# Loading tokens eight to a partition, and a grouped convolution in 20-row groups with two store queues

## The reference

```python
x = group_norm(x)                       # over groups of 4 channels, one scale and shift per image
x = x + window_attention(x)             # 8 heads, 8x8 windows with dilation 2, projection, roll
y = conv_general_dilated(x, w, (1, 1), 'SAME', feature_group_count=32) + b   # 3x3, NHWC
y = (y - mean(y, (0, 1, 2))) * rsqrt(var(y, (0, 1, 2)) + 1e-5) * gamma + beta
x = x + relu(y)
for w1, b1, w2, b2, w3, b3 in two_sets:  # two residual blocks of scanned 1x1, 3x3, 1x1 convolutions
    x = block(x)
```

## Time and profile before

| | |
|---|---|
| Median of three runs | 2432.0 us |
| Profiled execution, its own time | 2433.68 us |
| Its span in the trace | 2431.9 us |
| TensorE busy | 2062.5 us, 85% of the span |
| VectorE busy | 1672.6 us, 69% |
| ScalarE busy | 1166.5 us, 48% |
| GpSimd busy | 1068.4 us, 44% |
| Mean granted TensorE clock | 0.941 |
| DMA queue q1 | 239.09 MB, 32.5% of 16 engines' span |

### The profile page before, as it was taken

The page is one execution under the profiler, slowest core; times in us unless marked ns, Lnnn a source line. Parts: engine busy times, 40 slices in busy tenths (PEclk is TensorE's granted clock), DMA queues, the critical chain, the costliest instruction groups (busy, mean ns, idle before and its releaser), DMA issues. The chain is left out here.

```text
span 2431.9 us, 75176 instructions
## 1 busy us (share of the span) xinstructions
PE 2062.5 (85%) x30482; PEld 1083.4 (45%) x30482; DVE 1672.6 (69%) x3497; ACT 1166.5 (48%) x2603; POOL 1068.4 (44%) x1234
## 2 busy tenths in 40 slices
PE   5699989988998899859995377787999999999996
PEld 4455555555555555535553123232344443333332
DVE  5588999899899989962324665666667665655653
ACT  5577666666676676632222244333434443433430
POOL 0277777776777677749501442222112221111100
PEclk8799999999999999979997588898999999999997
DMA  8301111111111111112224655655444444444444
GB/s 229 105 26 46 48 34 48 37 47 33 49 35 48 34 48 36 48 43 72 94 95 172 233 184 145 212 172 173 124 140 131 136 133 106 130 118 120 121 100 104
DMA packets 259007, 243.82 MB, mean 100 GB/s; under 512 B 124784, under 2 KB 230512, under 8 KB 258672
## 3 DMA queue, kind: packets, MB, share of 16 engines
q1 hardware_dynamic: 258672, 239.09, 32.5%
HBM read 92.45 MB, written 89.65 MB: 75 GB/s over the span
## 5 line engine op out<-in xcount | busy, mean ns | idle before, releaser
L1226 POOL TENSOR_SCALAR l_x<-l_x,l_scale,l_shift 128x384 f32<-128x384 f32 x192 | 147.5, 770 | 573.8 <-PE banks L1644 573.8
L1602 PE MATMUL banks<-l_a,l_taps 128*32 128x384 f32 x3456 | 331.1, 517 | 60.2 <-ACT l_r L1298 60.2
L435 POOL TENSOR_TENSOR at_prob<-at_prob,at_inv 128x512 f32<-128x512 f32 x288 | 294.2, 1042 | 116.6 <-DVE at_inv L575 111.3
L501 ACT ACTIVATE at_prob<-at_prob 128x512 f32<-128x512 f32 x288 | 181.9, 632 | 307.4 <-DVE at_prob L565 307.4
L1617 PE MATMUL banks<-l_above,l_taps 128*32 128x384 f32 x1728 | 311.7, 494 | 11.3 <-ACT l_above L1313 9.8
L1309 ACT ACTIVATE l_above<-l_below 96x384 f32<-96x384 f32 x144 | 75.5, 524 | 510.5 <-issue 274.9
L1617 PE MATMUL banks<-l_below,l_taps 128*32 128x384 f32 x1728 | 310.7, 495 | 0.0
L617 PE MATMUL banks<-at_xn,at_w 128*64 128x256 f32 x2336 | 286.1, 387 | 1.8 <-ACT at_xn L453 1.4
L1602 PEld LDWEIGHTS banks<-l_a,l_taps 128*32 128x32 f32 x3456 | 122.2, 115 | 243.8 <-issue 243.8
L1474 DVE COPY l_old<-l_a 32x384 f32<-32x384 f32 x576 | 221.7, 385 | 11.5 <-DVE l_bias L1431 0.2
L656 PE MATMUL banks<-const,at_prob 128*128 128x128 f32 x1152 | 183.8, 287 | 51.2 <-POOL at_prob L435 50.1
(11 more groups left out here) (160 smaller groups left out, 3598.0 us busy)
## 6 DMA issues: line engine op xcount, KB each, us to landing
l_x<-both SPq DMA_DIRECT2D x48, 768.0 KB, 4.4
l_rows<-l_r SPq DMA_DIRECT2D x768, 48.0 KB, 2.0
l_work<-both SPq DMA_DIRECT2D x36, 768.0 KB, 5.5
at_k_bd<-at_k SPq DMA_DIRECT2D x584, 32.0 KB, 1.8
load_raw<-in_x SPq DMA_DIRECT2D x36, 512.0 KB, 5.0
both<-c_y SPq DMA_DIRECT2D x96, 192.0 KB
both<-l_x SPq DMA_DIRECT2D x24, 768.0 KB, 3.9
out<-l_x SPq DMA_DIRECT2D x24, 768.0 KB, 4.5
```

Source lines behind the costliest of these rows:

```text
L435: nc.gpsimd.tensor_tensor(prob[i][p][:, :, :], prob[i][p][:, :, :], inv[i][p][:, :].unsqueeze(2).broadcast_to([P, HEADS, WIN]), ALU.mult). ...
L501: nc.scalar.activation(prob[j % 2][p][:, :, :], prob[j % 2][p][:, :, :], ACT.Exp).then_inc(s["exped"], 1)
L1602: last = nc.tensor.matmul(grid(acc(k)[block_rows(c), :]), e[kind_of(k)][:, dy + 1, dx, :], a[:, k % A_RING, rows_, dx:dx + SIDE], start=(d ...
```

## The change

In the load stage each partition now takes eight consecutive tokens, 4 KB, in one piece. TensorE turns the same 288 blocks; ScalarE writes each bank to every eighth run of four tokens, so that `x_res` holds the tokens in order again; VectorE's statistics of a bank-sized piece wait for both halves of the span. The loops are written out, and eight PSUM banks are used in place of six. Attention's weights, bias and tables are loaded at the end of the load stage, on the same queue behind the spans, and attention's waits for them are gone.

In the grouped convolution a group has 20 rows (four tiles of 5 rows, 480 columns), the last of an image 16 rows; there are 5 groups per image, 20 in all. The stores of quarters 0 and 2 are given out by SyncE, those of 1 and 3 by ScalarE right behind its own copy. The weight preparation starts with group 0 in place of group 2.

```diff
-        x_v = x_dram.rearrange("(g i t p) c -> p i t g c", i=LOAD_RING, t=LOAD_T, p=P)
+        x_v = x_dram.rearrange("(g p t) c -> p g (t c)", t=LOAD_T, p=P)
...
-            sp.dma_start(sh.const[:, :], const_dram).then_inc(const_in, 16)
-            with sp.Fori(0, rounds) as g:
-                for i in range(LOAD_RING):
-                    sp.wait_ge(turned, g * CHUNKS + 2 * i + 2)
-                    sp.dma_start(raw[:, i], x_v[:, i, :, bass.ds(g, 1), :].rearrange("p t g c -> p (t g) c"))\
-                        .then_inc(raw_in[i], 16)
+            for n, (tile, dram) in enumerate(first_drams):
+                if n == 1:
+                    for g in range(spans):
+                        i = g % LOAD_RING
+                        if g >= LOAD_RING:
+                            sp.wait_ge(turned, 2 * (g - LOAD_RING + 1))
+                        sp.dma_start(raw[:, i].rearrange("p t c -> p (t c)"), x_v[:, g, :]).then_inc(raw_in[i], 16)
+                sp.dma_start(tile[:, :], dram).then_inc(late_in if n else const_in, 16)
+            sp.wait_ge(late_in, 16 * (len(first_drams) - 1))
...
-                    act.wait_ge(turned, chunk + 1 + CHUNKS)
-                    nc.scalar.activation(sh.x[:, bass.ds(chunk * BANK, BANK)], sh.bank[n][:, :],
-                                         ACT.Copy).then_inc(kept, 1)
+                act.wait_ge(turned, n + 1)
+                out = sh.x[:, g * LOAD_SPAN:(g + 1) * LOAD_SPAN].rearrange("p (n t) -> p n t", t=LOAD_T)
+                nc.scalar.activation(out[:, :, 4 * half:4 * half + 4],
+                                     sh.bank[n % 8].rearrange("p (t n) -> p n t", t=4), ACT.Copy).then_inc(kept, 1)
...
+            for n in range(2 * spans):
+                dve.wait_ge(kept, n // 2 * 2 + 2)
+                nc.vector.bn_stats(sh.stats[:, n * 6:(n + 1) * 6], sh.x[:, n * BANK:(n + 1) * BANK]).then_inc(counted, 1)
...
-            pe.wait_ge(s["w_in"], 48)
...
-    return g // 2 - 1 if g % 2 == 0 and 0 < g <= 2 * PREPARES else None
+    return g // 2 if g % 2 == 0 and g < 2 * PREPARES else None
...
-C1_ROWS = C1_T * TR
-C1_SPAN = C1_T * TILE
-C1_GROUPS = IMG // C1_SPAN
+C1_MOST = BANK // SIDE
+C1_ROWS = C1_T * C1_MOST
+C1_GROUPS = -(-SIDE // C1_ROWS)
+
+
+def c1_rows(g):
+
+    return min(C1_MOST, (SIDE - g % C1_GROUPS * C1_ROWS) // C1_T)
+
+
+def c1_span(g):
+    first = g // C1_GROUPS * IMG + g % C1_GROUPS * C1_ROWS * SIDE
+    return slice(first, first + C1_T * c1_rows(g) * SIDE)
...
-                for r in range(4):
+                for r in (0, 2):
                     sp.wait_ge(s["y_kept"], 4 * g + r + 1)
-                    sp.dma_start(y_dram[quarter(r), g * C1_SPAN:(g + 1) * C1_SPAN].rearrange("j (c n) -> c j n", c=C1_T),
-                                 y[:, g % Y_RING, r, :]).then_inc(y_out[g % Y_RING], 16)
+                    sp.dma_start(y_dram[quarter(r), c1_span(g)].rearrange("j (c n) -> c j n", c=C1_T),
+                                 y[:, g % Y_RING, r, 0:c1_rows(g) * SIDE]).then_inc(y_out[g % Y_RING], 16)
...
+                    if r % 2:
+                        act.wait_ge(s["y_kept"], 4 * g + r + 1)
+                        nc.scalar.dma_start(y_dram[quarter(r), c1_span(g)].rearrange("j (c n) -> c j n", c=C1_T),
+                                            y[:, g % Y_RING, r, 0:n]).then_inc(y_out[g % Y_RING], 16)
...
                     if n == len(taps) // 2 and prepare_at(g) is not None:
-                        pe.wait_ge(s["y_kept"], 4 * g)
+                        if g:
+                            pe.wait_ge(s["y_kept"], 4 * g)
+                        else:
+                            pe.wait_ge(s["tables"], 1)
...
-                link(nc.vector.bn_aggr(y_agg[:, r_, :], sh.stats[:, r_ * per_kind * 6:(r_ + 1) * per_kind * 6]))
+                link(nc.vector.bn_aggr(y_agg[:, r_, :], sh.stats[:, r_ * per_block * 6:(r_ + 1) * per_block * 6]))
```

More of the change, by code:

```diff
@@ L178, in _ @@
+            sp.wait_ge(late_in, 16 * (len(first_drams) - 1))
         @block.tensor
         def _(pe):
-            pe.sem_inc(turned, CHUNKS)
             pe.wait_ge(const_in, 16)
[L182 to L192, removed]
+            for n in range(2 * spans):
+                g, half = n // 2, n % 2
+                if half == 0:
+                    pe.wait_ge(raw_in[g % LOAD_RING], 16 * (g // LOAD_RING + 1))
+                wait(pe, kept, n - 7)
+                for t in range(4):
+                    last = nc.tensor.transpose(sh.bank[n % 8][:, t * P:(t + 1) * P],
+                                               raw[:, g % LOAD_RING, 4 * half + t, :], sh.const[:, C_ID:C_ID + P])
+                last.then_inc(turned, 1)
@@ L877, in _ @@
                     at = (r * groups + g) * 6
[L878 removed]
+                    nc.vector.bn_stats(sh.stats[:, at:at + 6], y[:, g % Y_RING, r, 0:c1_rows(g) * SIDE]).then_inc(s["counted"], 1)
         @block.tensor
@@ L905, in _ @@
                         for c in range(C1_T):
-                            top = C1_ROWS * at + TR * c
-                            r0, r1 = max(0, -dy - top), TR - max(0, top + TR + dy - SIDE)
-                            out = sh.bank[4 * (g % 2) + r][quarter(c), 0:TILE].rearrange("p (r c) -> p r c", c=SIDE)
+                            top = C1_ROWS * at + tall * c
+                            r0, r1 = max(0, -dy - top), tall - max(0, top + tall + dy - SIDE)
+                            out = sh.bank[4 * (g % 2) + r][quarter(c), 0:tall * SIDE].rearrange("p (r c) -> p r c",
+                                                                                               c=SIDE)
                             last = nc.tensor.matmul(
```

38 lines of the change are left out of this document (17 added, 21 removed).

## The result

The changed kernel takes 2411.97 us (median of four runs, 2410.91 to 2415.27) against 2430.97 us for the kernel before, a ratio of 0.9927 with a 95% interval of 0.9915 to 0.9940. It is faster by 19 us. The prediction was 2398 with a range of 2383 to 2413: the direction was right, the time lies at the range's upper edge (the ratio times the 2432.0 us that the forecast started from is 2414, just above it), and the gain is little more than half of the 34 us forecast. The profiled execution took 2415.27 us, its span 2413.5.

What follows compares the result with a forecast made beforehand. Load landing was taken as the load stage's largest part, TensorE as the convolution's pace with stores just beneath. Savings of 21.5 + 2.7 + 9.2 + 0.5 = 34 us off 2433.7, less 1.7, gave 2398, range 2383 to 2413.

Steps and rivals of the forecast that it cites:

- between them 512 KB gives 3.1, and I take 3.3 since three share the engines: Load stage: landing of a 512 KB load, interpolated from 2.9 us for 384 KB and 3.5 us for 768 KB.
- the 1.6 us kept: Load stage: turning, signals and stalls beside the landing in three span periods, taken to stay at 1.6 us.
- landing near 4.4 ... gives 2.0, which saves 7: Load stage, bound for a smaller gain: 2.0 us a span saves 7 us in place of 21.5.
- Rival 3: Load stage: landing stays near 5.0 us, 2.06 us a span, 6 us saved and not 21.5; 2413 us, chance 0.10.
- the DMA engines behind it are close to full: Load stage before the change: DMA engines 88% busy while moving only 241 GB/s.
- Attention's start: First projection: ScalarE waits only for three memsets, so TensorE starts at about 96.8, not 99.53; 2.7 us saved.
- Forecast 9.2: Convolution: net gain, TensorE ending 11.1 us earlier less 1.9 us for the last group's longer stores.
- stores run on four engines and that a second queue adds nothing: Convolution: DMA share of 0.26 means four engines of sixteen, set by the store's first dimension; two queues keep 0.26 to 0.28.
- The stated floor of 10.7 us: Convolution: stores of 18.9 MB take 194.6 us at 97 GB/s, so the end comes at most 10.7 us earlier.
- a group of nine 1.3 us more: 9.94: Convolution: with 480 columns a tap takes 0.145 us more, so a group takes 9.94 us in place of 8.63.
- 11.1 (13.6 less 2.5): Convolution: TensorE saves 13.6 us over four images, less 2.1 for a later start and 0.4 for cold taps.
- The scattered copies: Load stage: ScalarE's strided copies taken at 0.60 us each, 1.2 us a span, hidden under 1.63.

Runs made afterwards that it cites:

- e12: Probe ahead of the changed kernel's load stage: 4 KB packet loads nobody reads, one to five in flight; issues 3.47, 2.13, 1.58, 1.27 and 1.23 us apart.
- e3: The changed kernel with six load buffers in place of three: 2388.29 us, ratio 0.9833.
- e6: The changed kernel with 512-byte load packets, contiguous ScalarE copies and six load buffers: 2405.67 us, ratio 0.9906.
- e1: The changed kernel with all four stores of a convolution group given out by SyncE: 2411.73 us, ratio 0.9927.
- e2: The changed kernel with each convolution store split into four, one per tile, with 32 channels as first dimension: 2391.87 us, ratio 0.9842.
- e7: Groups of 16 rows (24 groups, 384 columns), all else as in e2: 2422.89 us, ratio 0.9974.
- e8: Groups of 12 rows (32 groups, 288 columns), all else as in e2: 2489.66 us, ratio 1.0244.
- e11: e8 with two semaphore signals nobody waits for behind each quarter of each tap, 72 a group: 2656.76 us, ratio 1.0963.

## Why the prediction was wrong

**The load stage is where it failed.** The step was "between them 512 KB gives 3.1, and I take 3.3 since three share the engines". The landing is 4.5 us, and 4.7 with nothing but loads [e12]. The form of the step was right, and so was the 1.6 us kept: with 4.5 us, (4.5 + 1.6) / 3 = 2.03 us a span, where 2.04 was measured. With six buffers a span of 1.33 and a landing of 6.5 leave 1.5 for the rest. So a term was mis-sized by 1.2 us, which is 0.4 us a span and 14 us in all. The landing of a load alone, 3.1 for 3.4 measured, was 0.3 of it, though one of the two rows behind it was a store (`both<-x_res`). The rest is sharing, to which I gave 0.2 us, as if loads hindered each other only with the engines full, near 411 GB/s; landing grows well before. The upper bound in the same paragraph, "landing near 4.4 ... gives 2.0, which saves 7", is what happened. Rival 3 at 2413, with a chance of 0.10, came within about 1 us of the result, but by luck: it had the landing at 5.0 and 1.17 us left, for 4.5 and 1.6 measured, errors that cancel, and too little gain in the convolution.

Its other premise, "the DMA engines behind it are close to full", was right only for small packets: 241 of 290 GB/s. With large ones the same ring leaves a third of the rate unused (264 of 410). The Trainium skill's rule that 512 bytes reach line rate ("DMA: Bandwidth & Descriptors", Specifications) is contradicted by e3 and e6, 410 against 290 GB/s with the engines full; but with three buffers the kernel came out almost as if it held.

**Attention's start.** 2.7 forecast, 2.4 measured.

**The convolution.** Forecast 9.2, measured 11.5, and the mechanism was half wrong: the number came near because the stores took back most of what TensorE gained beyond it. Right was that stores run on four engines and that a second queue adds nothing [e1, e2]. The stated floor of 10.7 us, made with 97 GB/s, is what decided; the stage gained 0.8 more. The two rules of the Trainium skill on engines and queues ("DMA: Bandwidth & Descriptors", Why a DMA increments its semaphore by 16 and not by 1; Issuing engines are not separate DMA queues) agree with the runs: 2411.7 us with one queue against 2412.0 with two, and a share of 0.43 once the first dimension was 32. Wrong was "a group of nine 1.3 us more: 9.94". TensorE's own work did grow with the columns, from 23 to 30 ns a product, 2.0 us a group; the error was to add the growth to a full period of 8.63 us. That period held idle time: TensorE had stopped for instructions. Over 190 us before the change its weight loads were idle 45.7 us for no releaser, over 150 us of e2 17.5, that is 0.24 and 0.12 of the time:

```profile
L909 PEld LDWEIGHTS banks<-x_res,c_w 32*32 32x32 f32 x6319 | 110.1, 103 | 76.5 <-issue 45.7
```

```profile
L918 PEld LDWEIGHTS banks<-x_res,c_w 32*32 32x32 f32 x4826 | 103.9, 103 | 42.6 <-issue 17.5
```

The added columns filled much of that wait. So once the stores are out of the way, 20-row groups save 31 us [e7 against e2], four periods of 8.88 less 4.6 for a first copy that comes later in its stage, where I had 11.1 (13.6 less 2.5). In the changed kernel the stores took half of the gain back: counted from the start of the second norm, TensorE's last product ended 24 us earlier than before (201.4 for 225.3), the stage 11.5.

**The rest.** The scattered copies cost nothing. ScalarE's issues took 1.28 us in the median, not 0.5, and between 1110 and 1280 us it idled 15.8 us behind them, but without them the time was the same [e1]. The statistics' combination went from 3.32 to 2.89 us. The tail's 1.1 us and attention's remainder are within what executions of one kernel differ by; I did not separate them.

What stays open: why landing grows with two and three loads in flight while the engines are not full, what sets the 3.7 to 4.0 us beat of the instruction blocks, and so whether something other than their transfer holds TensorE after every 128 pairs.

## What to carry to other kernels

Work out a ring's pace as (landing + time until the buffer is free again) / depth, with the landing measured at that depth; if the engines are not full at the rate that packets of this size can reach, a deeper ring is worth more than a larger packet. A DMA share that stays at 0.25 while several transfers of one kind are outstanding points to a shape that uses four engines: here changing its first dimension brought 20 us, changing its queue nothing. Before adding or scaling TensorE work per group, look for regular idle time after equal counts of instructions, for there fewer instructions pay, and columns are free until they fill the wait (here near 480).

## What was not expected of the hardware

- TensorE ran 127 or 128 weight loads and as many products, then stood still; blocks of 16 KB of instructions came every 3.7 to 4.0 us. By this, 288 products of 32 x 32 weights cost 8.9 us over 288 and over 384 columns [e8, e7], and hardly more over 480, where TensorE's own pace comes to 30 ns a product [e2].
- The landing of a 512 KB load grows from 3.4 us alone to 4.7 with three in flight, one load per 1.58 us; with a fourth they come every 1.27 us [e12].
- ScalarE's issue of a store took up to 5.12 us in place of 0.5 while the four engines were behind.
- Two signals of TensorE's own behind each quarter of a tap cost 73 ns each, at a granted clock of 0.57 to 0.61 (1.00 without them) [e11].
